# Attention and FP4 feed-forward on one core: a TensorE job between scores and value sums

## The reference

```
p = silu(x @ W1 + b1);  u, v, q, k = split(p, 4)       # 16 heads of 8
scores[h] = q[h] @ k[h].T                              # 2048 x 2048 each
av[h] = (silu(scores[h]) / 2048) @ v[h]
x1 = layernorm(x + layernorm(av * u, gamma, beta) @ W2 + b2)
h  = silu(fp4(x1) @ fp4(w_gate).T) * (fp4(x1) @ fp4(w_up).T)    # 352 wide
out = layernorm(x1 + fp4(h) @ fp4(w_down).T)
```

## Time and profile before

| | us |
|---|---|
| median of 3 runs (516.2 to 516.4) | 516.2 |
| the profiled execution | 516.33 |
| its span, first to last instruction | 514.2 |
| TensorE busy in it | 496.7 |
| ScalarE busy | 487.3 |
| VectorE busy | 285.8 |
| GpSimd busy | 81.4 |
| the 512 silus of the scores, busy | 474.8 |

### The profile page before, as it was taken

The page is one execution under the profiler, slowest core; times in us unless marked ns, Lnnn a source line. Parts: engine busy times, 40 slices in busy tenths (PEclk is TensorE's granted clock), DMA queues, the critical chain, the costliest instruction groups (busy, mean ns, idle before and its releaser), DMA issues.

```text
span 514.2 us, 20251 instructions
## 1 busy us (share of the span) xinstructions
PE 496.7 (97%) x9062; PEld 264.5 (51%) x9064; DVE 285.8 (56%) x730; ACT 487.3 (95%) x547; POOL 81.4 (16%) x180
## 2 busy tenths in 40 slices
PE   8899999999999999999999999999999999999996
PEld 5453335444344444434344444444477777777762
DVE  7644934655848375664847366573844433435445
ACT  4999999999999999999999999999999999999940
POOL 8413000102020200202020110202020202112010
PEclk9999999999999999999999999999999999999999
DMA  4732450000000000000000000000000000000000
GB/s 128 190 95 61 112 146 22 1 3 7 3 8 1 8 2 3 6 3 8 1 9 1 8 1 3 6 3 7 3 8 4 9 4 10 4 9 10 3 4 10
DMA packets 15173, 11.87 MB, mean 23 GB/s; under 512 B 1815, under 2 KB 14750, under 8 KB 15086
## 3 DMA queue, kind: packets, MB, share of 16 engines
q1 hardware_dynamic: 13800, 8.85, 6.5%
q0 software_dynamic: 704, 1.33, 0.9%
q10 hardware_dynamic: 582, 0.40, 0.3%
HBM read 1.92 MB, written 1.05 MB: 6 GB/s over the span
## 4 chain that ended last, share of the span: by engine, by line
ACT 51%; PE 28%; issue 17%; DVE 2%; DMA 1%; POOL 0%; POOLq 0%; SPq 0%; DVEq 0%
ACT attn L680 50%; PE ps L433 26%; PE ps L447 2%; DMA gate_b<-in_L_attn_b 1%; ACT feat L680 0%; ACT v_sb L680 0%; PE ps L467 0%; ACT uT L680 0%; POOL rstd_b L405 0%; DVE xn_b L817 0%; DVE stats_b L847 0%; DVE xn_b L825 0%; DVE xn_b L823 0%; DVE xn_b L821 0%; POOLq L136 0%
## 5 line engine op out<-in xcount | busy, mean ns | idle before, releaser
L680 ACT ACTIVATE attn<-ps 128x1024 f32<-128x1024 f32 x512 | 474.8, 1182 | 1.3 <-PE ps L433 0.8
L433 PE MATMUL ps<-attn,v_pad 128*32 128x256 f32 (+1 forms) x5120 | 274.4, 341 | 0.3 <-DVE wdown_t L1046 0.2
L433 PE MATMUL ps<-q_stack,k_stack 64*128 64x256 bf16 (+1 forms) x2560 | 172.9, 251 | 10.1 <-ACT attn L680 1.3
L433 PEld LDWEIGHTS ps<-attn,v_pad 128*32 128x32 f32 x5120 | 132.2, 109 | 80.3 <-issue 38.8
L433 PEld LDWEIGHTS ps<-q_stack,k_stack 64*128 64x128 bf16 x2560 | 79.0, 94 | 132.3 <-ACT attn L680 85.4
L404 POOL TENSOR_TENSOR ve_a<-mv_a,eps_col 128x1 f32<-128x1 f32 x24 | 4.6, 191 | 207.9 <-DVE mv_a L849 207.9
L404 POOL TENSOR_TENSOR ve_b<-mv_b,eps_col 128x1 f32<-128x1 f32 x24 | 4.6, 191 | 194.6 <-DVE mv_b L849 194.6
L433 PE MATMUL ps<-zeros 128*128 128x512 bf16 x49 | 13.9, 425 | 1.4 <-DVE zeros L973 1.2
L405 POOL TENSOR_TENSOR rstd_a<-ve_a,minus_half 128x1 f32<-128x1 f32 x24 | 13.5, 561 | 1.9
L405 POOL TENSOR_TENSOR rstd_b<-ve_b,minus_half 128x1 f32<-128x1 f32 x24 | 13.4, 560 | 1.9
L909 DVE COPY xqT<-ps 128x128 f32<-128x128 f32 x15 | 4.4, 292 | 16.2 <-PE ps L433 16.2
(11 more groups left out here) (189 smaller groups left out, 402.9 us busy)
## 6 DMA issues: line engine op xcount, KB each, us to landing
q_stack<-parts SPq DMA_DIRECT2D x18, 128.0 KB, 2.4
k_stack<-parts SPq DMA_DIRECT2D x12, 128.0 KB, 3.1
k_stack<-parts SPq DMA_DIRECT2D x15, 64.0 KB, 2.6
x_sb<-in_L_attn_x SPq DMA_DIRECT2D x3, 256.0 KB, 4.3
q_stack<-zeros SPq DMA_DIRECT2D x6, 128.0 KB, 2.5
k_stack<-parts POOLq DMA_DIRECT2D x9, 64.0 KB, 2.6
q_stack<-parts SPq DMA_DIRECT2D x8, 64.0 KB, 2.0
out<-x_a SPq DMA_DIRECT2D x8, 64.0 KB, 1.5
```

What stands on the lines that cost most here:

```text
L433: return pe.matmul(to, lhsT, rhs, start=start, stop=stop, skip_group_check=True)
L680: return act.activation(to, frm, ACT.Silu, **kw)
```

## The change

In the loop of TensorE the job of a step now stands directly behind the scores of that step, ahead of the value sums. Which jobs there are, their steps, banks and waits stay, as does every other engine's code. Steps 0 and 1 have no sums, and behind the loop nothing changes.

```diff
             for at in range(len(STEPS)):
                 scores(at)
+                if at in JOB_AT:
+                    job(at)
                 if at >= LAG:
                     times_v(at - LAG)
-                if at in JOB_AT:
-                    job(at)
             for at in range(len(STEPS) - LAG, len(STEPS)):
                 times_v(at)
```

## The result

The changed kernel takes 517.79 us (median of 15 runs, 516.57 to 520.33), the kernel before beside it 516.16 (15 runs, 514.81 to 516.55). By the medians that is 1.63 us. The ratio worked out from all executions is 1.0045, with a 95% interval of 1.0031 to 1.0058: slower by 1.6 to 3.0 us. Forecast were 517.5 and slower. The profiled execution took 519.48 us, 517.3 of it span, and so belongs to the upper group.

A forecast was written before the change was run, and what follows sets the result against it. ScalarE's activations were taken to bound the kernel. Terms 0.72 + 0.89 - 0.10 - 0.22 gave +1.29 us, 517.62 for the profiled execution and 517.5 for the median; range 516.4 to 518.6.

The forecast's parts named there:

- ScalarE sets the time: From first scores to last, ScalarE's activations set the time; TensorE's order costs only where ScalarE runs dry.
- The stall at step 2: First x transposes, moved ahead of the sums, wait 0.92 us for their x load; 0.72 us late, bounds 0 and 0.92.
- The stall at step 7: K projection one step behind a V job waits 1.52 us for ScalarE's read; 0.89 us late, bounds 0 and 1.07.
- The clock: TensorE's granted clock after a 1.5 us pause in the loop: taken at 0, upper bound 1.46 us.
- Hand-overs: Down jobs two steps into a chunk wait for VectorE's accumulator read, 0.04 us of room: taken at 0, bound 5 x 0.1.
- rival (b): Tight hand-overs missed: about 0.1 us at five chunk starts and five gate-to-up pairs, half absorbed; 518.0, chance 0.20.
- Waits that go: Sums at steps 34 and 242 no longer wait for VectorE's copy: gains of 0.10 and 0.22 us.
- Switches of tile shapes: TensorE's overlaps between tile shapes in the new order: taken at 0, bounds 0 and -0.12 each, about -0.5 in all.
- Rival (a): The x data is there in time, so the step 2 stall falls away: +0.57 us, 516.8, chance 0.18.

The follow-up runs named there:

- both_behind: The changed kernel, but the jobs of steps 2 and 7 stay behind the value sums: 516.12 us, ratio 1.0004.
- gains_only: The kernel before, with the job ahead of the value sums only at steps 33 and 241: 516.21 us, ratio 1.0000.
- losses_out: The changed kernel, but jobs at steps 2, 3, 7, 29 and two steps into a chunk stay behind the sums: 516.95 us, ratio 1.0015.
- x_load_early: The changed kernel with the load of x rows 1280 up issued before the stacking DMAs of K unit 3: 516.90 us, ratio 1.0017.
- k_behind: The changed kernel, but the job of step 7 (K projection) stays behind the sums: 518.81 us, ratio 1.0053.
- only_two_ahead: The kernel before, with the job ahead of the sums only at steps 2 and 7: 517.98 us, ratio 1.0049.
- spaced: The changed kernel with the K projection of step 7 at step 8 and the V job of step 9 at step 10: 516.54 us, ratio 1.0015.
- after_again: The changed kernel run once more, unaltered, on another chip; its profile is the second profile: 517.67 us, ratio 1.0032.

## Why the prediction was right

**ScalarE sets the time, and TensorE's order counts only where it runs dry.** Right: of the 3.56 us by which the last activation is late in the first profile, 3.1 are idle time ahead of the silus and 0.5 are in their lengths, and all of it comes at places that a single job makes.

**The stall at step 2.** Right in cause. The forecast had 0.72; the second profile, at full clock, shows 0.43, with x landing 0.36 us nearer to the first activation than in the trace of before. The load's landing isn't fixed by the program, so the size is right for the one landing that was read. One term was too small: the transposes start 0.14 us behind the landing in the profiles where they stand for it, and not 0.05. The job of step 3 isn't priced in the forecast. It costs nothing while that of step 2 stands ahead too, and 0.12 us at activation 5 in `both_behind`, where step 2 is put back and x is in time.

**The stall at step 7.** 0.89 forecast, 0.86 measured in every profile with the job ahead. The stall, forecast at 1.52, was 1.51 counted the same way (32.67 against the 31.16 at which the sums would have started), 1.44 of it idle.

**The clock.** This was costed at nothing, with a bound at step 7, where it never fell. It fell at the other pause, in one of the two profiles and, to judge by the two groups, in about half of the first 15 executions. The two profiles put its price, as an estimate, at 2.58 - 0.43 = 2.15 us, less about 0.6 for x landing later: some 1.5 us. That the median came out near the forecast all the same is luck. Eight of 15 executions lie in the lower group, and 517.79 is the slowest of these eight: with one more in the upper group the median would have been 518.76, above the range of 516.4 to 518.6.

**Hand-overs, rival (b).** Here 0 was taken with 0.04 us of room. The room isn't there: this wait, met directly behind scores and 0.15 us behind VectorE's end, costs 0.06 on TensorE and 0.04 on ScalarE at four chunk starts and 0.07 at the fifth. The sum is 0.24 us, and the gate-to-up pairs cost nothing; the rival had 0.1 in ten places, half of it absorbed.

**Waits that go.** -0.10 and -0.22 forecast, -0.10 and -0.20 measured. But `gains_only` shows that they belong to the whole group of moved jobs, not to two.

**The sum.** At full clock 1.29 us was forecast and 1.39 is measured in the second profile. Two errors cancel in this: step 2 came out 0.29 smaller, and places taken at 0 cost 0.38 (0.14 from step 29, 0.24 at the chunk starts).

**Switches of tile shapes.** The bounds were open only to the gain side. At step 29 the job ends in matmuls with one contraction row, and the sums follow them 0.07 us before their end (78.57 + 0.42 against 78.92), not 0.18 as sums and other strips do: 0.11 lost, and 0.03 more in the job's first group (0.43 against 0.40). TensorE, 77 to 80 us of the first profile:

```profile
78.23 0.40 PE L433 MATMUL ps<-w_sb,beta_mat 128*32 128x128 f32 x8
78.57 0.42 PE L433 MATMUL ps<-b_row,ones_row 1*32 1x128 f32 x8
78.92 1.07 PE L433 MATMUL ps<-attn,v_pad 128*32 128x256 f32 x16
```

The scores of step 30 come 0.14 later by this. ScalarE feels 0.10 at once and the other 0.04 at activation 33; in `losses_out`, with this job behind, both are gone. **Rival (a)**, x in time, is the kernel `x_load_early`: 516.9, against 516.8 worked out. That is 0.9 above the kernel before on the same chip and not 0.57, and its last activation is 0.95 late: the 0.38 of the places taken at 0 is in it too.

## What to carry to other kernels

On an engine that keeps its order, what stands directly ahead of a job is its cover. Before a job is moved up, write beside it when each thing that it waits for arrives, a load and the reader of its buffer included, and look first at jobs whose readers sit behind long instructions of the busiest engine. Jobs that feed each other keep their distance only if they move together: from activation 34 on the mixed order of `losses_out` lost 0.65 us where the full change in sum lost nothing. And a pause of 1.2 us at one place cost more by TensorE's clock (some 1.5 us, an estimate) than by itself, while one of 1.44 us at another place didn't touch the clock.

## What was not expected of the hardware

The granted clock fell to half behind pauses of 1.22, 1.88 and 2.12 us in a loop that was otherwise full of matmuls, and came back while the engine ran on (1.00 again from 24 us on in the first profile). Behind the pauses of 1.44 us at step 7 it stayed at 1.00. Executions of over 518.2 us were 7 of 15 in the changed kernel, 5 of 6 in `k_behind` and 2 of 6 in `only_two_ahead`, and none of 17 in the two kernels with zeros in the pause. But `spaced` and `after_again`, without zeros and on the same two chips as those, had none of 16 either (though one of `spaced`, 517.35 us, has a mean clock of 0.995), so what the zeros do for the clock is open; a pair of kernels with and without zeros on one chip where the clock falls wasn't run.

The load of x, issued at the same place of the program, landed between 3.75 us (`after_again`) and 5.3 us (`k_behind`) behind the start of the first activation.
